# Edge pass of a four-layer graph network: weighted matrices stored by ScalarE from its own queue, one step after their eviction, instead of by SyncE

## What is computed

```python
h = relu(layernorm(x))
# layer 0: a message for each edge, summed at its target
m   = relu(concat(h[src], h[dst], edge_attr) @ W1.T + b1) @ W2.T + b2
x   = x + norm(h + relu(segment_sum(m, dst) @ Wu.T + bu))
# layers 1 and 2: sums of h[src] over the edges of each target (counts)
# layer 3: the same sums with weights
norm = dinv[src] * w * dinv[dst]
out  = segment_sum((h @ W)[src] * norm[:, None], dst) + b
```

## Time and profile before

| what | us |
|---|---|
| median of three runs | 2399.5 |
| the profiled execution | 2400.12 |
| its span on the core | 2398.6 |
| first gather of the edge pass | 142.07 |
| first and last relu (L961) of the pass | 161.85, 1391.2 |
| matrix layers and norms behind it | to 2398.6 |

### The profile page before, as it was taken

One profiled execution on the slowest core, in us unless ns is written; L12 is line 12 of the kernel. 1 busy time (PEld: TensorE's weight loads), 2 busy tenths in 40 slices (PEclk: granted clock), 3 DMA queues, 4 the chain that ended last, 5 costly groups with the idle time before them and its releaser, 6 DMA issues. The chain is left out here.

```text
span 2398.6 us, 31354 instructions
## 1 busy us (share of the span) xinstructions
PE 1557.9 (65%) x10942; PEld 1012.2 (42%) x10942; DVE 957.5 (40%) x2738; ACT 659.2 (27%) x1639; POOL 900.3 (38%) x911
## 2 busy tenths in 40 slices
PE   1405555555555555555455553998978989599997
PEld 1303333434333333334333342675645556445544
DVE  5644454545445454545455446221322124301111
ACT  1303333333333333334333311121323332100000
POOL 5046666666666666666666622000000000000001
PEclk8655666665556666666666655998889989799999
DMA  6423434343443434343343432000100001594571
GB/s 160 119 62 101 119 104 124 109 125 106 112 119 103 124 109 125 107 121 109 106 123 107 121 111 59 1 1 8 41 15 2 5 9 33 191 332 174 200 270 60
DMA packets 203234, 247.43 MB, mean 103 GB/s; under 512 B 36541, under 2 KB 177416, under 8 KB 203061
## 3 DMA queue, kind: packets, MB, share of 16 engines
q1 hardware_dynamic: 174260, 184.35, 24.3%
q0 software_dynamic: 28800, 60.80, 9.7%
HBM read 174.04 MB, written 57.60 MB: 97 GB/s over the span
## 5 line engine op out<-in xcount | busy, mean ns | idle before, releaser
L809 POOL DMA_INDIRECT arena<-dram_PHL,src_of x806 | 823.8, 1022 | 495.0 <-issue 213.2
L1026 PE MATMUL psum<-arena 128*128 128x100 f16 x1568 | 220.9, 247 | 260.0 <-issue 215.0
L1026 PEld LDWEIGHTS psum<-arena 128*128 128x128 f16 x1568 | 174.7, 129 | 392.5 <-issue 370.5
L1010 PE MATMUL psum<-arena 128*128 128x128 f16 x1612 | 209.0, 288 | 180.7 <-issue 146.5
L961 ACT ACTIVATE arena<-psum 128x512 f16<-128x512 f32 x202 | 120.5, 596 | 649.5 <-remote 574.2
L1028 PE MATMUL psum<-arena 128*128 128x50 f16 x1568 | 213.3, 229 | 57.0 <-issue 56.5
L1010 PEld LDWEIGHTS psum<-arena 128*128 128x128 f16 x1612 | 147.6, 130 | 216.4 <-issue 215.8
L2275 POOL DMA_DIRECT2D parts_a<-dram_x x7 | 5.3, 763 | 609.1 <-POOLq L2473 586.0
L880 DVE SCALAR_TENSOR_TENSOR agg_all<-psum,agg_all 128x64 f32<-128x64 f32 x202 | 44.5, 221 | 403.2 <-remote 399.4
L1028 PEld LDWEIGHTS psum<-arena 128*128 128x128 f16 x1568 | 171.5, 114 | 71.1 <-issue 69.8
L869 DVE SCALAR_TENSOR_TENSOR arena<-psum,arena 128x512 f16<-128x512 f32 x202 | 138.4, 685 | 151.7 <-issue 103.8
(11 more groups left out here) (359 smaller groups left out, 2135.3 us busy)
## 6 DMA issues: line engine op xcount, KB each, us to landing
arena<-dram_aw SPq DMA_DIRECT2D x7, 6400.0 KB, 20.4
dram_aw<-arena SPq DMA_DIRECT2D x196, 200.0 KB
arena<-dram_aw SPq DMA_DIRECT2D x3, 4800.0 KB, 17.1
arena<-in_ea_quads SPq DMA_DIRECT2D x51, 256.0 KB
arena<-dram_rel SPq DMA_DIRECT2D x51, 256.0 KB
arena<-arena SPq DMA_DIRECT2D x408, 32.0 KB
arena<-dram_PHL,src_of POOLq DMA_INDIRECT x806
arena<-dram_aw SPq DMA_DIRECT2D x2, 4000.0 KB, 14.8
```

The source lines that it names most:

```text
L809: nc.gpsimd.indirect_dma_start(gathered_p[:, slot, k, :], None, d["PHL"], bass.IndirectOffsetOnAxis(ap=src_of[:, b:b + 1], axis=0)).then_i ...
L1010: nc.tensor.matmul(out[:, k * P:(k + 1) * P], side[:, s, at:at + P], node_side[:, g % NAB, part * D:(part + 1) * D], start=(part == 0 and ...
L1026: nc.tensor.matmul(out, hot_lo[:, u, p, :], hot_key[:, u, p, 0:2].rearrange("p a k -> p (a k)"), start=True, stop=False)
```

## The change

SP no longer stores; ACT does, with a DMA from its own queue between relu(s) and matrix_out(s - 1).

```diff
--- before.py
+++ after.py
@@ -770,10 +770,6 @@
-                def store_weights(r):
-                    sp.wait_ge(adj_out, r + 1)
-                    sp.dma_start(d["aw"][r], aw_out[:, r % 3, :]).then_inc(aw_stored[r % 3], 16)
-
...
@@ -786,8 +782,6 @@
                         if q + 2 < QUADS:
                             load_edges(q + 2)
-                    if 2 <= s < J + 2:
-                        store_weights(s - 2)
...
@@ -974,6 +968,10 @@
+                def store_weights(r):
+                    act.wait_ge(adj_out, r + 1)
+                    nc.scalar.dma_start(d["aw"][r], aw_out[:, r % 3, :]).then_inc(aw_stored[r % 3], 16)
+
...
@@ -982,6 +980,8 @@
                 for s in range(MG + 1):
                     if s < MG:
                         relu(s)
+                    if 2 <= s < J + 2:
+                        store_weights(s - 2)
                     if 1 <= s <= J:
                         matrix_out(s - 1)
```

## The result

In 20 runs of each, side by side, the changed kernel takes 2402.19 us in the median (2397.51 to 2404.89) and the kernel before 2398.8 (2393.44 to 2402.4): ratio 1.0015, 95% interval 1.0009 to 1.0021. That is no change by the 0.2% of the forecast. But the small difference that is there, +3.4 us, is clear of zero by this interval, and it lies on the other side of the forecast's -2. The profiled execution took 2399.38 us, its span is 2397.8.

The account below looks back on a forecast made before the run. The edge pass was taken as a chain of waits, paced by a two-step beat of gathers and late PE results. All terms were 0 except -2 us at the pass's end: 2398.1 us profiled, 2397.5 us median, range 2352 to 2412.

Parts of the forecast that it names:

- The landing wait at 0: ACT's 142 us wait before L967 for a landed store goes, but saves 0 because PE's sums are late anyway.
- The rivals that made it real (2255 and 2358 us): Store wait on the path: every quad shortens, about 2255 us (chance 0.09), or only 11 quads gain, 2358 (0.20).
- the 41 us of the 11 quads: Waits in quads where relu(4q+3) starts right behind ACT's own work: taken as 0, with 41 us as other bound.
- The beat that takes up delays: Edge pass: eight gathers, then about 2 us until PE's results are out; two steps take 12.02 us, delays absorbed.
- SP's issues and the transfers at 0: 196 issues, 104 us of SP's time, are off the path; the same 39 MB is spread over the quad: 0 us.
- The end of the pass at -2 us: Last store wait, 5.14 us at 1378.29, has no beat covering it: between 0 and 5.14 us come off, 2 taken.
- ScalarE's stores at 0: ACT's 196 added issues, 0.53 us each between relu and matrix_out, taken as 0 us.
- the 25 us of the other bound: Upper bound for ACT's issues: 48 x 0.53 us, one tight step a quad; twice that with a second.
- The rival that put ACT's issue on the path at full price (2424 us): Issue between relu(s) and matrix_out(s - 1) delays L974 by 0.53 us in each quad's tight step; ACT's issue rival, chance 0.10.
- The rival of disturbed gathers (2409 us): Stores in every step share DMA engines with gathers; one gather a quad 0.2 us longer costs 10 us; chance 0.08.
- what would show the forecast right: No L967 store wait, multiply(4q+3) right behind build, add(4q+1) 1.5 to 2 us after eight gathers, relu(13) to relu(193) about 1107 us.

Follow-up runs that it names:

- Six buffers: Kernel before with six buffers for the weighted matrices instead of three, stores still from SyncE: 2386.39 us against 2386.06, ratio 1.0000; repeated, 1.0001.
- a 294 us delay: Changed kernel with each store cut into four DMAs of a quarter, all from ScalarE: 2409.61 us, ratio 1.0043; the changed kernel beside it 2402.02.
- the mean of five: Changed kernel three times, store behind the eviction on ScalarE twice, against the kernel before: 1.0015, 1.0003, 1.0016, 1.0006, 1.0011; mean 1.0010.

## Why the prediction was right, and where it was wrong

**The landing wait at 0: right.** Six buffers take it away and the time stays (1.0000 and 1.0001). The rivals that made it real (2255 and 2358 us) are refuted, also the 41 us of the 11 quads in which relu follows ACT's own work (a count gives 12 quads and 44.0 us, 1.1 to 5.2 each, which changes nothing).

**The beat that takes up delays: right as a mechanism, too simple as a picture.** Results that come late together, a stretch of gathers, a pause: all of that is in the trace of after. The pauses are 18% of the time from 200 to 1380 us, and 115 of the 182 long waits of relu (over 1 us) end in one. 97% of a 294 us delay vanish in it. But its period is not set by GpSimd's slots, and a stretch of eight gathers is not a law: in the whole pass 71 of 122 stretches are of two groups and 48 of one, where they were 82 and 23 before (78 and 34 in a second execution of the kernel before).

**SP's issues and the transfers at 0: right.** Without any store in the pass a quad takes 24.38 us. Here the Trainium skill's rule that issuing from several engines saves only issue time ("DMA: Bandwidth & Descriptors", "Issuing engines are not separate DMA queues") gave the right order of size, 0. The measurement limits the rule: with half the gathers the same move of the issues brought 153.6 us, through the place of the store in SP's program.

**The end of the pass at -2 us: wrong, and it gave the forecast its sign.** The 5.14 us wait at 1378.29 was that execution's. In a second execution of the same kernel the last store wait is 2.24 us, and relu follows with 1.94 us of idling of its own:

```profile
1374.77 0.51 ACT L967 ACTIVATE arena<-psum 128x400 fp8e4<-128x400 f32 x1 [2.24 <-issue]
...
1379.31 0.60 ACT L961 ACTIVATE arena<-psum 128x512 f16<-128x512 f32 x1 [1.94 <-remote]
```

relu(193) to the last add took 27.5 us in the first and 24.7 in the second, and 24.9, 24.9 and 26.0 in three executions of the changed kernel. So by the pair of executions the term lies between about -2.6 and +1.3 us, in the mean at about -1, and no gain can be told from none. It was read from one row of one execution.

**ScalarE's stores at 0: too low, as far as is known.** The stated mechanism holds in the trace: 0.34 us beside a running relu, the eviction no later than before. The lower bound of 0 was taken for the issues, and 0 for the transfers. With the wait worth nothing, as six buffers show, what the moved stores cost is the whole difference: +3.4 us in the first comparison, +2.4 in the mean of five. That is a tenth of the 25 us of the other bound, but the sum had no term of that sign. Which part of the move costs it stays open. The rival that put ACT's issue on the path at full price (2424 us) is refuted, even four issues a step (+9.8 us against the kernel before) don't come near it. The rival of disturbed gathers (2409 us) isn't borne out either: from 200 to 1380 us a gather takes 1.012 us in the mean in the changed kernel and 1.023 in the kernel before. In the last session, where GpSimd's issue alone sets the pace, it is the other way round: 1.004 us with six buffers and 1.014 with the store behind the eviction on ScalarE, with quads of 20.95 and 21.11 us. That is one execution each, so there the rival is open.

Of what would show the forecast right, the store wait is gone, multiply(4q + 3) follows its build, and relu(13) to relu(193) is 1112.6 us instead of about 1107. add(4q + 1) comes about 2 us behind a stretch in 29 of 44 quads. In the quad shown it came 3.4 us behind; there add(100) started with the stretch's end, and relu(102) 1.6 us after it.

## What to carry to other kernels

Before a wait is taken away, look at the results that are due behind it: if they are already late for a reason of their own, the wait's time moves to the next wait and the total stays. A cheap proof is a version that removes the wait and nothing else (more buffers), and one that adds a delay at the same place; here they gave 0 us of 142, and 7.6 us of 294. A term of 2 us from a single row of one profiled execution is too small to give a forecast its sign.

## What the runs showed of the hardware

**GpSimd's gathers and TensorE's results.** While GpSimd streams indirect gathers, results of matmuls that were taken up long before come late, 8.3 us in the rows shown; with the same matmuls and plain DMAs, from SyncE or from GpSimd, they don't. That was expected as a possibility. What wasn't: it isn't a property of the program alone. In the last session, with the store runs repeated, the kernel before itself took 2211.7 us in the median of 23 runs (2206.89 to 2216.56), 7.8% less than the 2399.8 of the session ahead of it. It was the only session of the experiments on its chip; the others were on two other chips. The rows of the six-buffer kernel there, 200 to 1140 us:

```profile
L809 POOL DMA_INDIRECT arena<-dram_PHL,src_of x719 | 722.0, 1004 | 219.2 <-issue 219.2
L1015 PE MATMUL psum<-arena 128*128 128x512 f16 x358 | 153.9, 525 | 438.7 <-DMA arena<-dram_PHL,src_of 438.5
...
L961 ACT ACTIVATE arena<-psum 128x512 f16<-128x512 f32 x179 | 106.9, 597 | 535.1 <-PE psum L1015 533.6 <-issue 1.3
```

GpSimd never waits for a slot there, TensorE waits for the gathers' landing, and no result is late. A gather takes 1.004 us and 219.2 / 719 = 0.305 stand between two, so 16 of them are 20.9 us, and the quads take 20.95: there the pass is bound by GpSimd's issue alone. The start of the pass shows the two conditions with the same instructions. First relu(1) in that session, with six buffers, then in the kernel before, in the session ahead of it:

```profile
163.03 0.60 ACT L961 ACTIVATE arena<-psum 128x512 f16<-128x512 f32 x1 [1.84 <-PE psum L1015]
```

```profile
183.97 0.60 ACT L961 ACTIVATE arena<-psum 128x512 f16<-128x512 f32 x1 [22.32 <-remote]
```

GpSimd has its first 24 gathers under way in both. Why the results are late in one session and not in the other is open, and a difference between chips can't be told from one between sessions: the gathers are needed for it, but they are not enough. The two edits that were run under both conditions kept their ratios within the scatter (1.0000 and 1.0001, 1.0006 and 1.0011).

**Issue times.** A store of 128 x 1600 bytes takes ScalarE's queue 0.34 us to issue, SyncE's 0.49 in the mean; four quarters of it take ScalarE's 1.79 to 3.54 us, 2.06 in the mean.
